# A perceiver layer on one core: the expert stage's last down chunk in two products, its row transposes moved behind the h transposes, and its gathers issued three tiles ahead and ahead of the slot copies

## The reference, cut to what matters

```python
logits = xf @ w_router.T
top_w, sel = jax.lax.top_k(logits, TOP_K)             # TOP_K = 2 of 8 experts
top_w = jax.nn.softmax(top_w, axis=-1)
gates = zeros.at[arange(T)[:, None], sel].add(top_w)
for e in range(E):
    h = silu(xf @ w_gate[e]) * (xf @ w_up[e])         # 256 -> 704
    out = out + gates[:, e:e + 1] * (h @ w_down[e])   # 704 -> 256
```

## Time and profile before

| | |
|---|---|
| median of 3 runs | 1529.26 us (1528.14 to 1529.8) |
| time of the profiled execution | 1529.16 us |
| its span, first to last instruction | 1527.2 us |
| granted TensorE clock, mean | 0.969 |
| busy share of the span | PE 93%, weight loads 85%, DVE 74%, ACT 66%, POOL 55% |
| expert stage | from about 1005 us to the end |

### The profile page before, as it was taken

One profiled execution on the slowest core, in us unless ns is written; L12 is line 12 of the kernel. 1 busy time (PEld: TensorE's weight loads), 2 busy tenths in 40 slices (PEclk: granted clock), 3 DMA queues, 4 the chain that ended last, 5 costly groups with the idle time before them and its releaser, 6 DMA issues.

```text
span 1527.2 us, 53971 instructions
## 1 busy us (share of the span) xinstructions
PE 1422.5 (93%) x15668; PEld 1294.9 (85%) x15669; DVE 1125.5 (74%) x3967; ACT 1000.9 (66%) x2482; POOL 838.1 (55%) x1401
## 2 busy tenths in 40 slices
PE   6969999999999999999999999649999999999997
PEld 5858888888888888888888888449999999999997
DVE  3647777777777777777777777557877787787775
ACT  4726766767766766766766676237777777677674
POOL 4514655655655655565565554226665666566554
PEclk9969999999999999999999999569999999999999
DMA  5302544554333343343343331425555555556554
GB/s 187 81 12 81 167 140 130 165 159 128 110 103 90 98 114 90 88 119 88 97 117 86 87 81 41 180 78 160 143 162 140 155 145 160 138 144 161 137 141 111
DMA packets 102009, 183.81 MB, mean 120 GB/s; under 512 B 19392, under 2 KB 61376, under 8 KB 101792
## 3 DMA queue, kind: packets, MB, share of 16 engines
q1 hardware_dynamic: 86272, 164.35, 35.2%
q0 software_dynamic: 15680, 18.76, 7.0%
HBM read 152.63 MB, written 31.13 MB: 120 GB/s over the span
## 4 chain that ended last, share of the span: by engine, by line
PE 72%; DVE 8%; issue 6%; ACT 2%; DMA 2%; POOL 1%; POOLq 1%; DVEq 0%; ACTq 0%; SPq 0%
PE m L412 12%; PE k L412 10%; PE y_p L1420 9%; PE v_p L412 9%; PE up_p L1420 8%; PE gate_p L1420 8%; PE sc L412 7%; PE pt L471 5%; PE ht_p L1459 3%; DVE dtv L976 2%; DMA par<-zbuf,gi 2%; ACT wd L735 1%; PE m L493 1%; PE z_p L1426 1%; DVE kT L868 1%
## 5 line engine op out<-in xcount | busy, mean ns | idle before, releaser
L735 ACT ACTIVATE wd<-wd,nmx 128x257 f32<-128x257 f32 x512 | 254.7, 499 | 100.6 <-DVE nmx L879 97.2
L879 DVE CUSTOM_DVE_ANT_0 wd<-sc,wd 128x257 f32<-128x257 f32 x512 | 187.3, 422 | 56.1 <-PE sc L412 45.8
L1622 POOL DMA_INDIRECT out<-par,oi x71 | 113.5, 1599 | 146.7 <-ACT par L1528 146.1
L1249 POOL TENSOR_TENSOR ctx_lo<-wd,ctx_hi 128x516 fp32r<-128x516 f32 x128 | 165.3, 1291 | 48.9 <-ACT ctx_hi L711 44.1
L711 ACT ACTIVATE wd<-pt 128x512 f32<-128x512 f32 x256 | 151.5, 592 | 57.9 <-PE pt L471 57.7
L471 PE MATMUL pt<-con,wd 128*128 128x128 f32 x1024 | 161.0, 280 | 3.0 <-ACT wd L735 0.7
L412 PE MATMUL k<-ctx_hi,wkh 128*128 128x256 f32 x512 | 158.2, 309 | 1.4 <-POOL ctx_lo L1249 1.4
L412 PE MATMUL v_p<-wvh,ctx_hi 128*128 128x256 f32 x512 | 158.0, 309 | 0.5 <-ACT y L711 0.5
L1499 ACT ACTIVATE uw_hi<-wu 128x1408 fp32r x71 | 98.3, 1385 | 85.1 <-PE up_p L1420 84.8
L1610 POOL COPY oi<-par 128x4 int32 x71 | 148.2, 2088 | 0.0
L1557 DVE TENSOR_TENSOR uw_lo<-wu,uw_hi 128x1408 fp32r<-128x1408 f32 x71 | 115.4, 1626 | 41.2 <-ACT uw_hi L1499 41.2
(11 more groups left out here) (197 smaller groups left out, 4662.2 us busy)
## 6 DMA issues: line engine op xcount, KB each, us to landing
dl<-d_low SPq DMA_DIRECT2D x71, 768.0 KB, 4.4
wd<-in_ctx SPq DMA_DIRECT2D x128, 258.0 KB, 2.8
wd<-in_mask SPq DMA_DIRECT2D x512, 32.1 KB, 1.8
wd<-in_wd SPq DMA_DIRECT2D x24, 256.0 KB, 3.0
d_high<-wd SPq DMA_DIRECT2D x24, 256.0 KB, 2.0
d_low<-wd SPq DMA_DIRECT2D x24, 256.0 KB, 2.3
wd<-d_high SPq DMA_DIRECT2D x8, 768.0 KB, 9.1
wg<-in_wg SPq DMA_DIRECT2D x8, 704.0 KB
```

The source lines that it names most:

```text
L735: nc.scalar.activation(pr[:, g, :], sm[:, g, :], ACT.Exp, bias=nmx[:, g:g + 1], scale=-1.0, accum_out=rsum[:, g:g + 1]).then_inc(exp_done, 1)
L879: V.tensor_tensor_reduce(sm[:, g, :], SC[g][:, 0:S], msk[:, b, :], -1.0, 3.0e38, ALU.add, ALU.min, nmx[:, g:g + 1]).then_inc(max_done, 1)
L1249: G.tensor_tensor(ctx_lo[:, b % 2], ctx[:, b], ctx_hi[:, b % 2].bitcast(F32), ALU.subtract).then_inc(lo_done, 1)
L1622: G.indirect_dma_start(outd[:, :], bass.IndirectOffsetOnAxis(oi[:, s, 1:2].bitcast(U32), 0), yb[:, s, :], None, compute_op=ALU.add).then_i ...
```

## The change

The last chunk of the down product is stacked. Its 64 true columns of h stand twice in `hb` (a second, 64-column multiplication in `gate_up`), so that after the transpose rows 0 to 63 of `hT[0]`'s last chunk hold the high half, and rows 64 to 127 are overwritten by DVE with the low half. The down weights' last chunk is written twice as well: two DRAM to DRAM copies in SP's program behind `tile(28)` put rows 0 to 63 of `d_high` and `d_low` on rows 64 to 127. The chunk then takes two matmuls, one by the high weights and one by the low ones. The memset `blank` goes; `take_h` on DVE becomes three subtractions. PE's `turn_z(t+1)` moves from between gate and up to right behind `turn_h`, ahead of gate. On POOL the gather is for tile t+3 and stands first, ahead of `owners(oi, t-1)` and the scatter.

```diff
@@ -32,7 +32,7 @@
 DV = 4
 FH = F // 2
 NSLOT = (TOK * TOPK + E * (P - 1)) // P
-assert NSLOT % 2 == 1
+assert NSLOT % 2 == 1 and 2 * FL == P
 PIECE = 2 * D
 PIECES = E * FC * D // PIECE
 TPE = TOK // P
@@ -232,6 +232,7 @@
         RK = M[:, 2 * H:2 * H + E]
 
         raw_in, raw_high, raw_low, raw_out = sem("raw_in"), sem("raw_high"), sem("raw_low"), sem("raw_out")
+        twin_out = sem("twin_out")
         par_in, con_in, ctl_in, pad_in = sem("par_in"), sem("con_in"), sem("ctl_in"), sem("pad_in")
         wxbc_in = sem("wxbc_in")
         hi_done, lo_done, wh_done, wl_done = sem("hi_done"), sem("lo_done"), sem("wh_done"), sem("wl_done")
@@ -389,12 +390,17 @@
                 load_expert(i - 3)
             with sp.Fori(3 + E, 4 + PIECES) as i:
                 tile(i, i - 4)
-            for i in range(4 + PIECES, NT):
+            tile(4 + PIECES)
+            sp.wait_ge(raw_out, 32 * PIECES)
+            for parts in (d_high, d_low):
+                last_chunk = parts.rearrange("p (e c d) -> p e c d", e=E, c=FC)[:, :, FC - 1, :]
+                sp.dma_start(last_chunk[FL:P], last_chunk[0:FL]).then_inc(twin_out, 16)
+            for i in range(5 + PIECES, NT):
                 tile(i)
 
             sp.wait_ge(o_ready, B)
             sp.wait_ge(px_done, 2 * B)
-            sp.wait_ge(raw_out, 32 * PIECES)
+            sp.wait_ge(twin_out, 32)
             for e in range(E):
                 sp.dma_start(wd[:, e].rearrange("p c d -> p (c d)").bitcast(F32),
                              d_high[:, e * FC * D:(e + 1) * FC * D]).then_inc(wd_in, 16)
@@ -1345,7 +1351,7 @@
         hb = spare[1][:, 0:FC * P]
         assert spare[1].shape[1] >= FC * P
         zT = [sb(f"zT_{h}", [P, 2, NH, P], F32R) for h in ("hi", "lo")]
-        hT = [sb(f"hT_{h}", [P, FC, P], F32R) for h in ("hi", "lo")]
+        hT = [sb("hT_hi", [P, FC, P], F32R), sb("hT_lo", [P, FC - 1, P], F32R)]
         dl = sb("dl", [P, 2, FC, D], F32R)
 
         gw = [sb(f"gw_{h}", [P, 2, NH, F], F32R) for h in ("hi", "lo")]
@@ -1361,7 +1367,7 @@
         y_out = sem("y_out")
         zT_ready, zT_done = sem("zT_ready"), sem("zT_done")
         g_ready, u_ready, silu_done, h_done = sem("g_ready"), sem("u_ready"), sem("silu_done"), sem("h_done")
-        hT_ready, zT_high, blank = sem("hT_ready"), sem("zT_high"), sem("blank")
+        hT_ready, zT_high = sem("hT_ready"), sem("zT_high")
         hT_high, hT_done = sem("hT_high"), sem("hT_done")
         dl_in = [sem(f"dl_in{s}") for s in range(2)]
         gw_high, gw_done = sem("gw_high"), sem("gw_done")
@@ -1441,7 +1447,7 @@
 
             def up(t, s):
                 pe.wait_ge(uw_done, t + 1)
-                at_least(pe, h_done, t)
+                at_least(pe, h_done, 2 * t)
                 inner(UB, s, uw).then_inc(u_ready, 1)
 
             def inner(bank, s, w):
@@ -1452,22 +1458,27 @@
                 return last
 
             def turn_h(t):
-                pe.wait_ge(h_done, t + 1)
+                pe.wait_ge(h_done, 2 * t + 1)
                 for k in range(2):
-                    at_least(pe, hT_done, 2 * t)
+                    at_least(pe, hT_done, 3 * t)
                     for c in range(4 * k, min(4 * k + 4, FC)):
+                        if c == FC - 1:
+                            pe.wait_ge(h_done, 2 * t + 2)
                         last = nc.tensor.transpose(HB[k][:, (c % 4) * P:(c % 4 + 1) * P], hb[:, c * P:(c + 1) * P], ident)
                     last.then_inc(hT_ready, 1)
 
             def down(t, s):
                 e = nc.tensor.value_load(expert_of(t), min_val=0, max_val=E - 1)
-                pe.wait_ge(hT_done, 2 * t + 2)
+                pe.wait_ge(hT_done, 3 * t + 3)
                 pe.wait_ge(dl_in[s], 16 * (turn(t, s) + 1))
                 at_least(pe, y_done, t)
-                for c in range(FC):
-                    last = product(YB[:, 0:D], [h[:, c, :] for h in hT],
-                                   (wd[:, bass.ds(e, 1), c, :].rearrange("p o n -> p (o n)"), dl[:, s, c, :]),
-                                   c == 0, c == FC - 1)
+                def weights(c):
+                    return wd[:, bass.ds(e, 1), c, :].rearrange("p o n -> p (o n)"), dl[:, s, c, :]
+
+                for c in range(FC - 1):
+                    product(YB[:, 0:D], [h[:, c, :] for h in hT], weights(c), c == 0, False)
+                for k, w in enumerate(weights(FC - 1)):
+                    last = mm(YB[:, 0:D], hT[0][:, FC - 1, :], w, False, k == 1)
                 last.then_inc(y_ready, 1)
 
             def body(t, s, first=False, last=False):
@@ -1475,15 +1486,14 @@
                     turn_z(t, s)
                 else:
                     turn_h(t - 1)
-                gate(t, s)
                 if not last:
                     turn_z(t + 1, 1 - s)
+                gate(t, s)
                 up(t, s)
                 if not first:
                     down(t - 1, 1 - s)
 
             pe.wait_ge(wd_in, 16 * E)
-            pe.wait_ge(blank, 1)
             tiles(pe, body)
             turn_h(NSLOT - 1)
             down(NSLOT - 1, 0)
@@ -1492,7 +1502,7 @@
         def _(act):
             def silu(t):
                 act.wait_ge(g_ready, t + 1)
-                at_least(act, h_done, t)
+                at_least(act, h_done, 2 * t)
                 nc.scalar.activation(sg[:, :, :], GB[:, :, 0:FH], ACT.Silu).then_inc(silu_done, 1)
 
             def high(dst, src, done):
@@ -1576,11 +1586,13 @@
                 at_least(dve, hT_ready, 2 * t)
                 V.tensor_tensor(hb[:, 0:F].rearrange("p (f n) -> p f n", f=2), sg[:, :, :], UB[:, :, 0:FH], ALU.mult
                                 ).then_inc(h_done, 1)
+                V.tensor_tensor(hb[:, F:FC * P], sg[:, 1, FH - FL:FH], UB[:, 1, FH - FL:FH], ALU.mult).then_inc(h_done, 1)
 
             def take_h(t):
                 dve.wait_ge(hT_high, 2 * t + 2)
                 low(flat(hT[1][:, 0:4, :]), HB[0][:, :], flat(hT[0][:, 0:4, :]), hT_done)
-                low(flat(hT[1][:, 4:FC, :]), HB[1][:, 0:2 * P], flat(hT[0][:, 4:FC, :]), hT_done)
+                low(hT[1][:, 4, :], HB[1][:, 0:P], hT[0][:, 4, :], hT_done)
+                low(hT[0][FL:P, FC - 1, :], HB[1][FL:P, P:2 * P], hT[0][FL:P, FC - 1, :], hT_done)
 
             def body(t, s, first=False, last=False):
                 if not first:
@@ -1593,7 +1605,6 @@
                     split_up(t + 1)
 
             dve.wait_ge(info_done, 1)
-            V.memset(hb[:, F:FC * P], 0.0).then_inc(blank, 1)
             split_gate(0, 0)
             take_z(0, 0)
             split_up(0)
@@ -1623,24 +1634,25 @@
                                      yb[:, s, :], None, compute_op=ALU.add).then_inc(y_out, 16)
 
             def body(t, s, first=False, last=False):
+                if not last:
+                    gather(t + 3, 1 - s)
                 if not first:
-
                     owners(oi[:, 1 - s, :], t - 1, oi_done)
-                if not last:
-                    gather(t + 2, s)
-                if not first:
                     scatter(t - 1, 1 - s)
 
             pool.wait_ge(info_done, 1)
             pool.wait_ge(tab_in, 16)
             gather(0, 0)
             gather(1, 1)
+            gather(2, 0)
             body(0, 0, first=True)
             body(1, 1)
             body(2, 0)
-            with pool.Fori(3, NSLOT - 2, 2) as t:
+            with pool.Fori(3, NSLOT - 4, 2) as t:
                 body(t, 1)
                 body(t + 1, 0)
+            body(NSLOT - 4, 1)
+            body(NSLOT - 3, 0, last=True)
             body(NSLOT - 2, 1, last=True)
             body(NSLOT - 1, 0, last=True)
             owners(oi[:, 0, :], NSLOT - 1, oi_done)
```

## The result

The changed kernel takes 1555.96 us (median of 4 runs, 1553.98 to 1557.11) against 1528.7 us of the kernel before beside it. The ratio is 1.0177, 95% interval 1.0159 to 1.0195: 27 us slower. The forecast was 1570, slower, by 41 us. The direction and the mechanism came; the size was two thirds of what was forecast. The profiled execution has a span of 1552.9 us, 25.7 more than before.

A forecast was written before the change was run, and what follows sets the result against it. PE bounds quiet tiles, but a loop over ACT, DVE and POOL was to take over: 1529.16 us, +50.0 (65 tiles), -0.6 (five tiles), -12.0 (old waits), +4 (late gathers), making 1570.6, called 1570; 8-in-10 range 1526 to 1592.

The forecast's parts named there:

- POOL's order closes a loop: Expert stage: oi copy behind the gather is held by uw_lo, delays take_y, closing a loop over ACT, DVE, PE; +50.0 us.
- The tie: POOL's oi copy starts at 1133.25 or so, DVE's uw_lo at 1133.26; one late gather enters the loop; from the start 0.68.
- The loop's length: One tile around the loop over ACT, DVE and POOL: 7.64 us against 6.873, bounds 7.45 and 7.90.
- Late gathers: Four POOL gathers starting inside uw_lo each make the oi copy some 1.0 us later: +4 us, bounds 0 and +6.
- Old waits gone: PE's waits for gathered rows in the expert stage go with the gather a tile further ahead: -12.0 us.
- (e): Clock rival: PE idles near 1 us a tile in the loop, granted clock kept at 1.00; given no time of its own.
- Two products: PE's last chunk of the down product saves one matmul, 0.119 us by 71 tiles: -8.4 us while PE is the bound.
- DVE's pieces: DVE's split subtraction (+0.14 us) and second multiplication (0.21) are hidden by its waits for ACT: 0; uncovered, 24 us.
- (a): Rival: loop entered later, at the first late gather, tile 16 or 17: 1557.5 us; chance 0.12.
- (b): Rival: the oi copy always gets in ahead of uw_lo, so the loop never starts: 1508.8 us; chance 0.10.
- (c): Rival: the loop never starts, but gathered rows are as late as before: 1520.8 us; chance 0.04.
- (d): Rival: loop left each time; a blocked copy costs 0.77 us in some 27 tiles, cancelling 20.4 gained: 1529; chance 0.06.

The follow-up runs named there:

- (2): Kernel before with POOL's part of the change alone (gathers three tiles ahead and first in the order): 1538.18 us, ratio 1.0056.
- (1): Changed kernel with POOL's oi copy ahead of the gather again, gather still three tiles ahead: 1510.16 us, ratio 0.9869.
- (4): Changed kernel with DVE's uw_lo subtraction issued as two instructions of 704 columns: 1512.39 us, ratio 0.988.
- (7): Changed kernel with five extra 64-column DVE multiplications in each tile, ahead of the 64-column piece, results unused: 1506.73 us, ratio 0.9859.
- (8): Changed kernel with two extra 64-column DVE multiplications in each tile, ahead of the 64-column piece, results unused: 1569.13 us, ratio 1.0271.
- experiment 5: Kernel before with gathers three tiles ahead alone, oi copy ahead of the gather as before: 1520.14 us, ratio 0.995.
- (6): Changed kernel with the oi copy ahead of the gather, gather three ahead, and z turned between gate and up: 1508.88 us, ratio 0.9873.
- (3): Changed kernel with POOL's program and the z turn as before, so the stacked chunk alone: 1529.15 us, ratio 0.9994.
- experiment 9: Changed kernel with POOL's program as before (gather two ahead, oi copy ahead of it), z still turned behind h: 1562.16 us, ratio 1.0223.

## Why the prediction was right, and where its sizes were off

**POOL's order closes a loop: shown.** Entered in tile 2, kept up to tile 67, made by POOL's order alone (2), undone by the swap (1), by splitting the subtraction (4), and by moving the subtraction 0.65 us (7) but not 0.26 us (8).

**The tie: right, but in part by luck.** The prediction had the copy at 1133.25 and `uw_lo` at 1133.26, no reason for either side in one tile, and 0.68 for the loop from the start, as any one loss enters it. In tile 2 the copy came 1.85 us behind the end of `gw_lo` and not 1.81, and `uw_lo` 1.73 behind it and not the quiet tile's 1.82; so DVE won by 0.12. With 1.85 for the copy, DVE would win a quiet tile too, but by 0.03 only. The 1.73 could have been read before: in the same tile of the kernel before `gw_lo` starts at 1033.68 and `uw_lo` at 1037.03. That one late gather is enough to enter the loop, which the prediction held against the copy's side, did not come. In experiment 7 four scatters come 0.8 to 1.4 us late and no copy is held, as the gi copy ends with `gw_lo` all the same. Had the copy won in tile 2 and in the tiles after it, the time would have been near 1507 to 1510 us, as in 7 and 1, and not 1556.

**The loop's length: the mis-sized term.** Forecast 7.64 us with bounds of 7.45 and 7.90, measured 7.38 (1205.37 to 1220.13 is 14.76 us for two tiles of the gi copy). That is under the lower bound too, and the tiles of 7.33 and 7.44 us in turn are under the 7.5 to 7.8 that the prediction named as the sign of the loop. By its parts: `gw_lo` to `gate_up` 1.99, `uw_lo` 1.62, and the copy's end 0.04 are as forecast; ACT's start, an estimate that no row of before showed, is 0.10 as estimated; `gate_up` with its piece is 0.93 for 0.98. The one that was off is `take_y` to `gw_lo`: 2.91 forecast, 2.65 and 2.75 measured. I took the quiet tile's distance. The whole difference lies on ACT ahead of `gw_hi`: from `take_y` to it are 1.39 us in the quiet tile, and 1.11 (1210.37 to 1211.48) or 1.23 in the loop. That ACT waits for h's transposes in the quiet tile, and finds them long done in the loop, would explain it; no row shows such a wait, so this is argued. 65 tiles by 7.385 - 6.873 is +33.3, not +50.0.

**Late gathers: wrong in place.** I gave four of them +4 us. The gaps still come, 0.8 to 1.35 us over the usual wait, but ahead of the scatter. Timelines of POOL and DVE, changed kernel:

```profile
1146.06 1.62 POOL L1633 DMA_INDIRECT out<-par,oi  x1 [2.27 <-issue]
1147.12 1.18 POOL L1621 COPY gi<-par 128x4 int32 x1
...
1434.60 3.02 POOL L1633 DMA_INDIRECT out<-par,oi  x1 [2.82 <-issue]
...
1440.88 0.21 POOL L1621 COPY oi<-par 128x4 int32 x1
...
1434.52 1.62 DVE L1567 TENSOR_TENSOR gw_lo<-wg,gw_hi 128x1408 fp32r<-128x1408 f32 x1 [0.17 <-ACT gw_hi L1509]
```

The gi copy behind it is shorter by what the scatter is late (1.18 for 1.98), as it would have waited for `gw_lo` anyway, so three of the four cost nothing. The fourth started 0.08 us behind `gw_lo` and took 3.02 us in place of 1.61. All of POOL behind it was late, the oi copy came only behind the end of `uw_lo` (1439.06), free and still too late, and the tile cost 2.0 us; the loop went on in the next one. So the sum with measured terms is 33.3 - 0.6 - 12.0 + 2.0 = +22.7, and the stage shows +23.1.

**Old waits gone, -12.0: shown**, by the changed kernel's waits and by experiment 5. But the prediction's account of these 12.0 us is not whole: PE's waits for rows are 7.8 of them. Most of the rest lies behind the two longest waits, where the clock fell. PE stood 2.20 us until 1298.94; the windows of the kernel before around it are

```profile
1290.00:1298.00 8.00, 6.73 (x49) 6.45 (x47) 6.40 (x7) 5.72 (x9) 5.97 (x6) 1.00 0.58 173
1298.00:1306.00 8.00, 7.06 (x42) 7.07 (x43) 3.66 (x4) 2.77 (x5) 1.89 (x4) 0.79 0.22 41
```

In the loop PE idles some 0.5 us in each tile, and the granted clock of 1060 to 1520 is 1.00, as (e) had it.

**Two products, -8.4: shown** between experiments 5 and 6, 11 us with the spread of 5 (their traces' tiles are 6.87 and 6.72 us, so 0.15 and not 0.119 each); alone it gives nothing (3). The changed kernel gets none of it, as forecast. **z behind h, 0: shown** (6); eight transposes put the next matmuls back by 0.87 us (1039.05 to 1040.08, less 0.16), with 0.88 forecast. **DVE's pieces, 0 when PE is the bound: shown** (1); in the loop they are on its path, and two pieces more cost 13 us where 0.26 by 65 is 17. Their tile is 7.63 us, 0.25 more, and the tile of the late scatter loses 0.9 us less there. **SP's copies, 0:** nothing in the profile speaks against it, and experiments 1, 6 and 7, which have them, take 1510.2, 1508.9 and 1506.7 us where the sum with nothing for them is 1508.8; they weren't tried alone.

Of the rivals, (a) is out, as the loop is there from tile 2. (b), that the copy always wins, would have been 1508.8; experiment 7, in which it does, takes 1506.7, and the order swapped back 1510.2. (c) is out by experiment 5, and (d) as the loop is not left before tile 67.

## What to carry to other kernels

A small operation that feeds an engine in the middle of a tile has two prices: its own time, and the hold by an instruction of another engine that started first. Moving it is safe only if it still ends ahead of its reader when the longest such hold falls on it; and if the reader's own engine feeds the holder, look for a closed loop. Add it up from the work on its path and not from a quiet tile's distances, which can contain waits that the loop has not. Where the result hangs on a tie, read it in the tile in which it is first played, as a quiet tile can lie 0.1 us off: here the two sides are some 1507 and 1556 us. Before an order is changed to get one DMA out earlier, see whether the DMA's distance (here a tile more ahead) already buys all of it: three ahead with the old order takes everything, 1510 us against 1556.

## What the runs showed of the hardware

POOL's 128x4 copy takes 0.20 us free and is held to the end of a DVE subtraction of two SBUF operands that started first, be it by 0.12 us; one that is 0.11 us ahead isn't (experiments 2 and 7). Between two such subtractions in a row it gets in (experiment 4). A gather under way when one starts isn't slowed: 1.00 us at 1208.13, with `uw_lo` from 1208.61. One that starts 0.07 us behind it is the earlier trace rows, and so is a scatter that starts 0.08 behind: 3.02 us for 1.61. DVE's instructions with PSUM as one operand hold nothing that these rows show: with five such pieces in a row (experiment 7) the copy took 0.20 us beside them.

PE's waits for rows in the midst of steady matmuls are followed by a lower granted clock: 0.79 in the 8 us that hold a wait of 1.87 us (experiment 3), 0.79 in the 8 us behind one of 2.20 us (the kernel before), and 0.60 in the 8 us that hold the end of one of 4.31 us (experiment 9). With a wait of 0.78 us, and with 0.5 us of idling in each tile of the loop, it stayed at 1.00.
